# Pre-converted output-projection weights, loaded on another queue, and a final store in two halves: a latent-attention plus mixture layer on eight cores

## The reference, cut to what matters

```python
q_c  = rms_norm(x @ wq_down.T) * q_norm_w              # 1536
q    = concat(q_c @ wq_up.T, rope(q_c @ wq_rope.T))    # 16 heads of 128 + 64
kv_c = rms_norm(x @ wkv_down.T) * kv_norm_w            # 512
k, v = split(kv_c @ wkv_up.T)                          # k also gets rope(x @ wk_rope.T)
out  = softmax(causal(q @ k.T * scale)) @ v            # 16 heads of 128
x    = layernorm(x + out @ wo.T)
g, u = x @ gate.T, x @ up.T                            # 8192 shared, 1024 routed
ffn  = (silu(g) * u) @ down.T                          # the routed part times a weight per token
x    = layernorm(x + ffn)
```

## Time and profile before

| | |
|---|---|
| two runs | 4105.85 and 4504.19 us, median 4305.02 |
| the profiled execution | 4107.22 us |
| its span, first to last instruction, slowest core | 4106.0 us |
| spans of the 8 cores | 4041.2 to 4106.0 us |
| TensorE busy | 3104.9 us, 76% |
| DVE, ACT, POOL busy | 1452.2, 890.8, 318.5 us |
| attention stage on the slowest core | 869.9 to about 2042 us |
| output projection to the end of its matmuls | about 2042 to 2200 us |

### The profile page before, as it was taken

How to read it: one execution, slowest core, us unless ns; L and a number is a source line. 1 busy time by engine, 2 the same in 40 slices (tenths; PEclk the granted TensorE clock), 3 DMA queues, 4 the chain that set the end, 5 groups by cost and what they waited for, 6 DMA issues and landing times.

```text
span 4106.0 us, 39565 instructions; the slowest of 8 cores (4041.2 to 4106.0 us)
## 1 busy us (share of the span) xinstructions
PE 3104.9 (76%) x14108; PEld 1354.6 (33%) x14338; DVE 1452.2 (35%) x2079; ACT 890.8 (22%) x1083; POOL 318.5 (8%) x377
## 2 busy tenths in 40 slices
PE   2667344567887878788566469999999999999982
PEld 0223111122433334334222024444444444444430
DVE  2112334436555555655513322121222212222144
ACT  0111011226444554545402200000000000000021
POOL 1001100000000000000010000111111111110100
PEclk9989677776777677668687689999999999999985
DMA  9034732015334353523582355949567495664802
GB/s 132 1 53 65 101 54 32 15 25 103 60 66 96 69 98 60 103 55 64 116 154 25 43 54 49 100 56 90 65 60 89 48 101 72 62 82 42 103 1 82
DMA packets 716976, 281.59 MB, mean 69 GB/s; under 512 B 662257, under 2 KB 695537, under 8 KB 716658
## 3 DMA queue, kind: packets, MB, share of 16 engines
q0 software_dynamic: 405776, 181.69, 37.6%
q1 hardware_dynamic: 311010, 97.35, 11.5%
HBM read 348.99 MB, written 18.87 MB: 90 GB/s over the span
## 4 chain that ended last, share of the span: by engine, by line
PE 62%; DVE 13%; DMA 11%; issue 6%; ACT 4%; SPq 2%; another core or an unknown queue 1%; POOL 0%; DVEq 0%; ACTq 0%; POOLq 0%
PE pdnE L1336 12%; PE puE L1301 11%; PE pgE L1293 11%; PE pOC L926 4%; DMA Pt<-P 4%; PE paC L855 3%; PE pkvB L596 3%; PE paC L851 3%; DVE smx L883 3%; PE pdD L1099 3%; PE paC L789 3%; DMA wuE<-su 3%; PE paC L762 2%; PE pqcA L329 2%; SPq L911 1%
## 5 line engine op out<-in xcount | busy, mean ns | idle before, releaser
L1293 PE MATMUL pgE<-x1b,wgE 128*128 128x512 bf16 x2256 | 523.0, 382 | 23.4 <-DMA wgE<-sg 18.9
L1301 PE MATMUL puE<-x1b,wuE 128*128 128x512 bf16 x2259 | 520.4, 380 | 14.0 <-DMA wuE<-su 11.6
L1336 PE MATMUL pdnE<-O_sb,wdE 128*128 128x512 bf16 x2258 | 506.2, 384 | 26.3 <-issue 24.0
L1312 DVE CAST usE<-puE 128x512 bf16<-128x512 f32 x144 | 99.6, 692 | 856.7 <-ACT gsE L1308 496.9
L1308 ACT ACTIVATE gsE<-pgE 128x512 bf16<-128x512 f32 x144 | 86.0, 597 | 1409.8 <-PE puE L1301 1205.7
L851 PE MATMUL paC<-K,qnC 128*128 128x512 bf16 x544 | 284.5, 523 | 127.1 <-ACT S L868 74.4
L883 DVE TENSOR_REDUCE smx<-S 128x1 f32<-128x4096 f32 (+7 forms) x128 | 326.8, 2553 | 26.0 <-DVE S L875 17.0
L1336 PEld LDWEIGHTS pdnE<-O_sb,wdE 128*128 128x128 bf16 x2304 | 227.3, 99 | 305.2 <-issue 41.5
L1293 PEld LDWEIGHTS pgE<-x1b,wgE 128*128 128x128 bf16 x2304 | 226.5, 99 | 298.9 <-issue 32.8
L1301 PEld LDWEIGHTS puE<-x1b,wuE 128*128 128x128 bf16 x2304 | 225.7, 98 | 286.6 <-issue 17.7
L815 ACT ACTIVATE P<-S,smn 128x4096 bf16<-128x4096 f32 (+7 forms) x128 | 283.3, 2213 | 155.2 <-DMA Pt<-P 150.0
(11 more groups left out here) (193 smaller groups left out, 2350.6 us busy)
## 6 DMA issues: line engine op xcount, KB each, us to landing
wgE<-sg POOLq DMA_DIRECT2D x64, 512.0 KB, 9.0
wuE<-su POOLq DMA_DIRECT2D x64, 512.0 KB, 10.3
wdE<-sd POOLq DMA_DIRECT2D x64, 512.0 KB, 17.0
xkB<-xf POOLq DMA_DIRECT2D x8, 2048.0 KB, 17.7
xsum<-xo SPq DMA_DIRECT2D x1, 8192.0 KB, 43.6
woD<-wo POOLq DMA_DIRECT2D x16, 512.0 KB, 6.7
out<-xsum SPq DMA_DIRECT2D x1, 8192.0 KB, 22.0
wqd_sb<-wqd POOLq DMA_DIRECT2D x1, 6144.0 KB, 68.8
```

The costliest lines, as they stand in the source:

```text
L1293: i = ten.matmul(pg[w][:], wg_sl[sl][:, dc * 128:(dc + 1) * 128], x1b[:, dc * TOK + tt * 512: dc * TOK + tt * 512 + 512], start=(dc == 0), ...
L1301: i = ten.matmul(pu[w][:], wu_sl[sl][:, dc * 128:(dc + 1) * 128], x1b[:, dc * TOK + tt * 512: dc * TOK + tt * 512 + 512], start=(dc == 0), ...
L1336: i = ten.matmul(pdn[w][:], wd_sl[dsl][:, oc * 128:(oc + 1) * 128], h_buf[:, ic2 * TOK + tt * 512: ic2 * TOK + tt * 512 + 512], start=(ic2 ...
```

## The change

Three things. First, a DRAM tensor `wo_bf` is added, and at the head of the attention stage, ahead of its first loads, POOL issues one DMA that converts all of `wo` to bf16 into it. Second, the 16 loads of `woD` read `wo_bf`, are issued by SP, and the first of them waits for the conversion; their slots have semaphores of their own. Third, `emit_ln` notes the count of `s_ln` after each half, and the output is stored by two DMAs, each waiting for its half.

```diff
+    wo_bf = nc.dram_tensor("wo_bf", [D, D], BF16, kind="Internal").ap()
...
+            s_wocv = pswd()
+            s_wocv.inc(gps.dma_start(wo_bf, wo_), 16)
             load_wkg(0)
             load_q(0)
             load_wkg(1)
...
+                ln_tt_at[tt] = s_ln.n
...
-            s_wo = [pswd() for i in range(3)]
+            s_wo = [sem(f"s_woD{i}") for i in range(3)]
...
-            wo_r = wo_.rearrange("(c p) o -> p c o", p=128)
+            wo_r = wo_bf.rearrange("(c p) o -> p c o", p=128)
...
-                s_wof[sl].wait(gps)
+                s_wof[sl].wait(syn)
+                if i_ == 0:
+                    s_wocv.wait(syn)
                 s_wo[sl].inc(
-                    gps.dma_start(wo_sl[sl][:].rearrange("p (c o) -> p c o", c=NDC),
+                    syn.dma_start(wo_sl[sl][:].rearrange("p (c o) -> p c o", c=NDC),
                                   wo_r[:, :, i_ * 128:(i_ + 1) * 128]), 16)
...
-            s_ln.wait(syn)
-            i = syn.dma_start(out_.rearrange("(c p) t -> p c t", p=128),
-                              xsum[:].rearrange("p (c t) -> p c t", c=NDC))
-            s_out.inc(i, 16)
+            out_r = out_.rearrange("(c p) t -> p c t", p=128)
+            xs_r = xsum[:].rearrange("p (c t) -> p c t", c=NDC)
+            for tt in range(2):
+                syn.wait_ge(s_ln.h, ln_tt_at[tt])
+                i = syn.dma_start(out_r[:, :, tt * 512:(tt + 1) * 512],
+                                  xs_r[:, :, tt * 512:(tt + 1) * 512])
+                s_out.inc(i, 16)
```

More of the change, by code:

```diff
@@ L977, in build_nc @@
         s_ln = sem("s_ln")
+        ln_tt_at = {}
         def emit_ln(tag, to_x1b):
```

## The result

The changed kernel is slower by 1.5%: the ratio of its time to that of the kernel before is 1.015, with a 95% interval of 1.0132 to 1.0169. The profiled execution took 4168.03 us against 4107.22 before; the forecast was 4164.

What follows compares the result with a forecast made beforehand. TensorE was taken to carry 62% of the chain, DMA 11%. Terms of 70.8 - 4 + 0 - 10 = +57 on 4107.2 gave 4164 us, slower by 1.4%, with 4120 to 4215 for 8 in 10.

Steps and rivals of the forecast that it cites:

- term 1: Head of the attention stage: the wo conversion on POOL's queue holds loads behind it; +70.8 us, bounds +37 and +103.
- term 2: Start of the output projection: first woD load, half as large, stands behind xsum on SP; TensorE starts earlier, -4 us.
- What bounds the kernel: TensorE carries 62% of the chain, DMA 11%; the change acts only at attention start, projection start and last store.
- Term 3: Projection's other fifteen woD loads: bf16 halves their bytes, but they were hidden already; 0, at worst +14 us.
- Term 4: Last store in two halves: the first runs beside LayerNorm, the second needs 11.7 us instead of 22.0; -10 us.
- The sum: Whole kernel: 70.8 - 4 + 0 - 10 = +57, giving 4164 us, slower by 1.4%; chance 0.45.
- (a): Attention head: the conversion's writes ride free beside its reads, +46 in term 1, 4139 us; chance 0.25.
- (b): Attention head: slow conversion, both directions at a lone xkB's rate, 106.2 us, total 4196, slower by 2.2%; chance 0.2.
- (c): Attention head: the conversion does not hold the loads behind it and ends under the stage, 4093 us; chance 0.04.
- (d): Projection: 256-byte loads on SP run slower than TensorE takes them, +14 in term 3, total 4187 us; chance 0.06.

## Why the total came near, and which step was off

The forecast, slower by 1.4%, stands against 1.5% measured (1.3 to 1.7), and the time of the profiled execution lies 4 us above it. The mechanism was right; what failed is the size of term 1, and the way by which term 2 was to gain. By its steps:

- **What bounds the kernel.** Right. Only the three places named changed; the other pieces of the table moved by 3 us or less.
- **Term 1, that the loads behind the conversion wait.** Right, and shown: with the conversion behind them, or a stage earlier, the wait is gone.
- **Term 1, its size: this step failed.** It came to +75.5 us in the mean of the cores and +76.7 from slowest core to slowest, for +70.8 forecast. From the first issue to the first K build matmul the forecast had 79.3 us (1.5 + 74.2 + 3.1 + 0.5); measured were 82.6 in the mean, 76.7 until the conversion had landed and 5.9 from there. So the 75.7 us for the conversion were short by 1.0, and the 3.6 behind it, for the wkgC load by its bytes and the start, by 2.3; the other 1.4 is in what was taken off, 8.5 us on core 6 where the mean of the cores before is 7.1. The rule, reads and writes against one limit, was right, shown by the float32 copy and the casts to SBUF and DRAM. The rate of 339 GB/s from wqd_sb was nearly so: 335 in the mean, 321 on the slowest core.
- **Term 2.** -3.1 us in the mean for -4 forecast; on the slowest core alone it reads +1.1. The number was right in part by luck. The step had xsum landing 37.3 us after its issue, for having fewer bytes beside it, and 4 us more to the first matmul. In the mean xsum landed after 41.1 us (43.6 before), 12.58 MB at 306 GB/s and not at 337, and the first matmul came 2.4 us later: the first error costs 3.8 us, the second gives 1.8 back, and what they are taken off is 46.6 us in the mean, not core 6's 45.5. What the step also missed is that VectorE's wait for xsum stood close behind, so that the weights alone could bring little more: 6 us from the issue of xsum to the last matmul in the kernel that loads them on POOL.
- **Term 3.** 0, as forecast: matmuls 112.2 us for 112.4. The 256-byte loads land in 4.3 us, near the row of SP's small packets and far from POOL's.
- **Term 4.** -9.6 for -10, also by itself.
- **The sum.** In the mean of the cores the terms and the rest come to +62.8 for +57. That the profiled execution lies within 4 us is luck in part: from core 6 before to core 2 after, terms 1 and 2 together are 11 us above the forecast, and the attention stage from K build to xsum, taken as unchanged, is 8.8 us shorter (1164.0 to 1155.2), where the mean of all cores moved by 2.0.
- **What can be told.** The prediction took 2%, 82 us, as the least that can be told from no change. The interval of the ratio is 0.2% to either side, so the 1.5% are a clear loss; "within 2%", to which the prediction gave 0.74, came true and doesn't say so.
- **Rivals.** (a), writes that ride free: excluded, +24 us for 8.39 MB more of them. (b), slow conversion: excluded, 80.2 us on the slowest of the 8 cores where it needed more than 99. (c), loads not held: excluded, the first wkgC load landed 84.4 us after its issue. (d), slow small loads: excluded, 4.3 us against the pace of 6.9. The claim in term 1 that nothing covers the conversion is true at that place, and a stage earlier everything covers it.

Rival (c) priced a conversion that runs on under the attention stage at nothing. The kernel with the conversion behind the loads shows that this costs 24 us there, in one held transpose.

## What to carry to other kernels

Look at what stands behind a bulk transfer in its queue: a transfer for a later stage costs its whole length if the next stage's first load is behind it, and nothing if it is issued where the queue has been idle (here 141 us, visible in the waits) and lands before the next stage starts; issued just behind the stage's first loads it still cost 24 us. Price a DRAM to DRAM pass by the sum of what it reads and writes, and read its length on all cores, not on one (70.2 to 80.2 us here). And when a load is brought forward, ask which other load the consumer waits for: here weights, attention output and residual had to come in the right shape and order together before the projection started 14 us sooner.

## What the runs showed of the hardware beyond that

- One DMA transpose on SP's queue beside a bulk conversion on POOL's took 23 to 39 us, on each of 8 cores in two kernels (31.2 and 34.2 on the slowest core of each); in the kernel before none took more than 9.6.
- SP's first woD instruction, of 2048 runs of 256 bytes, stood 26.9 us in its issue (the SP timeline row above; 0.42 us is what xsum's took), 19.8 to 26.9 over the cores, with xsum's large load in the queue ahead and its semaphores long reached. Here nothing else stood behind it on SP; elsewhere it would delay what does.
- The GB/s slices of 193 to 207 beside 14 to 28 during the conversion don't show bursts. The view books a packet's bytes in the slice in which it starts, and the 256 packets of 32 KB written last some 4.9 us each (78.4 us on 16 engines), two slices of 2.4 us; in rows of 8 KB, with 2048 packets of 4 KB, nearly all slices until its last read 97 to 138.
